# The order of three matrix products per tile: from hi/hi pairs first to equal weights in a row

## The chip, the cores and the metric

The kernel runs on one core of a Trainium2 chip. The metric is the device time of one execution in microseconds (us). An adjacency matrix of 4096 by 4096 float32 streams from the chip's main memory through the core in chunks of 512 by 512 (1 MB each), 192 chunks in all. TensorE (PE) multiplies, ScalarE (ACT) and VectorE (DVE) prepare the operands, and the queue of SyncE (SP) issues the loads.

## The reference

```python
def reference(x, adj, d_list, weight, filt, bias, W_in, W_out):
    # layer 0: U = Vt = adj
    scale = sum(d_list * filt * d_list, axis=0)
    o = adj @ (scale[:, None] * (adj @ (x @ weight))) + bias
    x = layernorm(x + o)
    # layer 1
    a_in  = adj   / where(deg_row > 0, deg_row, 1)
    a_out = adj.T / where(deg_col > 0, deg_col, 1)
    x = layernorm(x + a_in @ x @ W_in + a_out @ x @ W_out)
    return x          # 4096 x 128, float32
```

Four products with the large matrix are needed: two in layer 0 and two in layer 1, each of 4096 x 4096 by 4096 x 128.

## The kernel before, in words

**Precision.** TensorE takes operands in a reduced float32 form. A float32 number is therefore split into a high part and a low part, x = x_hi + x_lo, and for the matrix raw = hi + lo. A product is taken as x_hi hi + x_lo hi + x_hi lo; the fourth term is dropped. ACT makes `hi` by copying `raw` into the reduced form (lines 204 and 207; line 207 also sums the rows). DVE makes `lo` as raw - hi (line 295).

**Tiles.** A chunk has four tiles of 128 x 512 and is worked on in two slabs of two tiles. The x side (128 x 128, `r_hi` and `r_lo` in the code) is the stationary operand, which is loaded as weights; the matrix tile (128 x 512) is streamed. A call of `product` is one chunk: two slabs of six matmuls, all of which add into one accumulator, `accA` or `accB`. There are 256 calls, that is 512 slabs and 3072 large matmuls.

**Stages.** The 192 chunks come in four phases. Phase 1 (64 chunks) makes z = adj x for each block of 512 rows, and as soon as a block's v (z times the layer's weight and scale) is there, the second product v adj goes beside it (`propagate`, `diagonal`). Phase 2 (28 chunks) finishes the second product, and normalises x block by block, with one part of layer 1 (`convolve2`). Phase 3 (64 chunks) is the other direction of layer 1 (`block3`, most of it in a loop that stays a loop in the program). Phase 4 (36 chunks) finishes layer 1, and writes each block of the output (`out_block`, `normalize` on DVE).

**What sets the order.** Each engine has its own order, written out by hand, and waits on counting semaphores. `raw`, `hi` and `lo` are rings of four chunks. The load of chunk n waits until DVE has made `lo` of chunk n-4. ACT's `hi` of chunk n waits for the load and until PE has released chunk n-4 (`s_rel`). DVE's `lo` waits for `hi`. PE waits for `hi` of a slab (`s_hi`) and for its `lo` (`s_lo`). A few small products (lines 485 and 486) and transposes (line 505) stand between the large ones. An instruction carries one wait itself; where it needs two, a separate wait instruction stands ahead of it in PE's program.

Of the kernel before, what the change touches and what calls it, by code (L numbers as in the profile page):

```python
# [12 lines left out]
TPB = 4  # L13
# [10 lines left out]
def graph_kernel(nc, x_t, adj_b, adjT_b, coef_t, W0, bias, W_in, W_out, ident_d, out):  # L24
# [62 lines left out]
    with ExitStack() as ctx:  # L87
        def sb(name, shape, dt=F32):
            return ctx.enter_context(nc.sbuf_tensor(name, shape, dt))
# [8 lines left out]
        hi = sb("hi", [P, RING, TPB, BLK], F32R)  # L98
# [364 lines left out]
        def _(pe):  # L463
            def product(acc, r_hi, r_lo, K, n, first, last, slot=None):

                slot = n % RING if slot is None else slot
                for s in range(SLABS):
                    tiles = range(TPS * s, TPS * s + TPS)
                    pe.wait_ge(s_hi, SLABS * n + (s + 1))
                    for t in tiles:  # L470
                        nc.tensor.matmul(acc, r_hi[:, TPB * K + t], hi[:, slot, t],  # L471
                                         start=(first and t == 0), stop=False)
                        nc.tensor.matmul(acc, r_lo[:, TPB * K + t], hi[:, slot, t], start=False, stop=False)  # L473
                    pe.wait_ge(s_lo, SLABS * n + (s + 1))
                    for t in tiles:
                        mm = nc.tensor.matmul(acc, r_hi[:, TPB * K + t], lo[:, slot, t], start=False,  # L476
                                              stop=(last and t == TPB - 1))
                return mm
# [17 lines left out]
            def diagonal(I):  # L496
                pe.wait_ge(s_v, I + 1)
                product(accB[:, I % 2], v_hi, v_lo, I, NB * I + NB - 1, I == 0, True).then_inc(s_rel, 1)
# [10 lines left out]
            def convolve2(n):  # L509

                J, I = chunks[n]
                pe.wait_ge(s_x1, NB - J)
                if J == NB - 1 and NB - 3 - I > 0:
                    pe.wait_ge(s_ys, NB - 3 - I)
                product(accA[:, I % 2], x_hi, x_lo, J, n, J == NB - 1, J == I + 1).then_inc(s_rel, 1)

            def propagate(n):

                J, I = chunks[n]
                pe.wait_ge(s_v, J + 1)  # L520
                if J == 0 and I >= 2:
                    pe.wait_ge(s_os, I - 1)
                product(accB[:, I % 2], v_hi, v_lo, J, n, J == 0, False).then_inc(s_rel, 1)
# [114 lines left out]
```

## Time and profile before

| | |
|---|---|
| Median of 3 runs | 768.69 us |
| Lowest and highest | 765.61 and 770.52 us |
| Profiled execution, span from first to last instruction | 767.6 us |
| PE busy | 740.5 us (96%), 3352 matmuls, 3352 weight loads |
| DVE busy | 581.9 us (76%) |
| ACT busy | 473.7 us (62%) |
| DMA | 206.48 MB, 269 GB/s on average |
| Granted TensorE clock, mean | 0.995 |

The page gives no other time for the profiled execution than its span, which lies 1.1 us under the median of the runs. A matmul's record begins before the one ahead of it has ended, since they are pipelined; so the distance from one start to the next (called the step below) is what counts, and not the duration. "PEld" rows are the weight loads, which run beside the matmuls. In a timeline, a bracket gives the idle time of the engine ahead of a row and what ended it.

### The profile page before, as it was taken

The page shows a single profiled execution, that of the slowest core. Times are in us where ns is not written, and L with a number is a line of the kernel's source. Part 1 is how long each engine was busy: PE and PEld are TensorE (multiplying, and loading weights), DVE is VectorE, ACT ScalarE, POOL GpSimd, SP SyncE. Part 2 cuts the span into 40 slices and gives each one's busy share as a digit, 9 for nine tenths or more (in the row PEclk, how much of TensorE's full clock was granted, in tenths as well). Part 3 has the DMA queues.
Part 4 walks back from the last instruction along what each step waited for, and adds up shares of the span by engine and source line. Part 5 has one row for each costly group of instructions (what it writes and reads, how often), then busy time and mean ns, then how long its engine had stood idle before and what let it go on. Part 6 is the DMA issues. An engine that isn't in the chain of part 4 may idle for free.

```text
span 767.6 us, 9866 instructions
## 1 busy us (share of the span) xinstructions
PE 740.5 (96%) x3352; PEld 608.2 (79%) x3352; DVE 581.9 (76%) x879; ACT 473.7 (62%) x1209; POOL 0.2 (0%) x4
## 2 busy tenths in 40 slices
PE   5999999999999999899999999999999999989994
PEld 4678888888888888688888888888888888877883
DVE  5897865938373558976566569888889899999986
ACT  6975866646454343333333368898889887556652
POOL 0000000000000000000000000000000000000000
PEclk9999999999999999999999999999999999999999
DMA  9977957656456273355555558899999999799991
GB/s 342 412 301 284 362 196 316 227 212 273 165 202 237 70 315 109 115 215 193 191 189 195 185 199 317 344 367 368 365 360 378 373 348 369 270 313 357 352 346 30
DMA packets 33929, 206.48 MB, mean 269 GB/s; under 512 B 3424, under 2 KB 8288, under 8 KB 9312
## 3 DMA queue, kind: packets, MB, share of 16 engines
q1 hardware_dynamic: 33888, 205.96, 71.4%
q8 instruction: 23, 0.38, 0.2%
q14 instruction: 18, 0.15, 0.0%
HBM read 203.85 MB, written 2.10 MB: 268 GB/s over the span
## 4 chain that ended last, share of the span: by engine, by line
PE 74%; DVE 17%; DMA 5%; ACT 1%; issue 1%; SPq 1%; DVEq 0%; ACTq 0%
PE accB L476 14%; PE accB L471 14%; PE accB L473 14%; PE accA L476 10%; PE accA L471 10%; PE accA L473 10%; DVE lo L295 10%; DMA raw<-in_adjT_b 5%; PE nat L486 2%; DVE rows L363 2%; DVE stats L346 1%; DVE rows L399 1%; ACT hi L207 1%; ACT hi L204 1%; DVE mv L349 1%
## 5 line engine op out<-in xcount | busy, mean ns | idle before, releaser
L295 DVE TENSOR_TENSOR lo<-raw,hi 128x1024 fp32r<-128x1024 f32 x384 | 457.9, 1223 | 101.9 <-ACT hi L207 52.6
L207 ACT ACTIVATE hi<-raw 128x512 fp32r<-128x512 f32 x512 | 315.7, 619 | 101.0 <-PE accB L476 74.5
L471 PE MATMUL accA<-hi,x_hi 128*128 128x512 f32 x512 | 203.4, 397 | 9.2 <-ACT hi L207 8.9
L473 PE MATMUL accA<-hi,x_lo 128*128 128x512 f32 x512 | 200.7, 392 | 0.0
L204 ACT ACTIVATE hi<-raw 128x1024 fp32r<-128x1024 f32 x128 | 127.9, 1051 | 95.7 <-PE accA L476 65.7
L476 PE MATMUL accA<-lo,x_hi 128*128 128x512 f32 x512 | 160.4, 395 | 5.9 <-DVE lo L295 5.8
L471 PEld LDWEIGHTS accA<-hi,x_hi 128*128 128x128 f32 x512 | 96.9, 189 | 31.3 <-issue 8.9
L476 PEld LDWEIGHTS accA<-lo,x_hi 128*128 128x128 f32 x512 | 95.4, 189 | 31.9 <-DVE lo L295 12.7
L473 PEld LDWEIGHTS accA<-hi,x_lo 128*128 128x128 f32 x512 | 97.0, 189 | 19.5
L471 PE MATMUL accB<-hi,v_hi 128*128 128x512 f32 x256 | 100.6, 393 | 0.1
L473 PE MATMUL accB<-hi,v_lo 128*128 128x512 f32 x256 | 100.3, 392 | 0.0
L471 PE MATMUL accB<-hi,x_hi 128*128 128x512 f32 x256 | 100.3, 392 | 0.0
L473 PE MATMUL accB<-hi,x_lo 128*128 128x512 f32 x256 | 99.7, 390 | 0.0
L207 ACT ACTIVATION_READ_ACCUMULATOR hi<-raw 128x1 f32 (+1 forms) x512 | 95.7, 187 | 0.0
L476 PE MATMUL accB<-lo,v_hi 128*128 128x512 f32 x256 | 79.9, 394 | 2.5 <-DVE lo L295 2.5
L476 PE MATMUL accB<-lo,x_hi 128*128 128x512 f32 x256 | 78.9, 389 | 0.0
L476 PEld LDWEIGHTS accB<-lo,v_hi 128*128 128x128 f32 x256 | 48.2, 189 | 13.4 <-DVE lo L295 3.4
L471 PEld LDWEIGHTS accB<-hi,v_hi 128*128 128x128 f32 x256 | 48.3, 189 | 10.9 <-DVE v_lo L326 0.6
L473 PEld LDWEIGHTS accB<-hi,v_lo 128*128 128x128 f32 x256 | 48.4, 189 | 9.8
L476 PEld LDWEIGHTS accB<-lo,x_hi 128*128 128x128 f32 x256 | 48.1, 188 | 10.0
L473 PEld LDWEIGHTS accB<-hi,x_lo 128*128 128x128 f32 x256 | 48.1, 188 | 9.7
L471 PEld LDWEIGHTS accB<-hi,x_hi 128*128 128x128 f32 x256 | 48.1, 188 | 9.7
(54 smaller groups left out, 244.1 us busy)
## 6 DMA issues: line engine op xcount, KB each, us to landing
raw<-in_adjT_b SPq DMA_DIRECT2D x128, 1024.0 KB, 6.0
raw<-in_adj_b SPq DMA_DIRECT2D x64, 1024.0 KB, 6.9
rows<-in_x_t SPq DMA_DIRECT2D x8, 256.0 KB, 9.8
out<-rows SPq DMA_DIRECT2D x8, 256.0 KB, 5.9
coef<-in_coef_t SPq DMA_DIRECT2D x1, 96.0 KB, 7.5
w<-in_W SPq DMA_DIRECT2D x1, 64.0 KB, 7.0
w_in<-in_W_in SPq DMA_DIRECT2D x1, 64.0 KB, 6.9
w_out<-in_W_out SPq DMA_DIRECT2D x1, 64.0 KB, 6.7
```

The source lines that it names most:

```text
L204: last = nc.scalar.activation(hi[:, slot, at], raw[:, slot, at], ACT.Copy)
L207: last = nc.scalar.activation(hi[:, slot, t], raw[:, slot, t], ACT.Copy, accum_out=sums[:, TPB * K + t, bass.ds(C, 1)])
L295: nc.vector.tensor_tensor(lo[:, slot, at], raw[:, slot, at], hi[:, slot, at], ALU.subtract).then_inc(s_lo, 1)
L346: last = nc.vector.bn_stats(stats[:, t], rows[:, TPB * I + t])
L349: last = nc.vector.bn_aggr(mv[:, t], stats[:, t])
L363: last = nc.vector.tensor_scalar(rows[:, TPB * I + t], rows[:, TPB * I + t], mv[:, t, 0:1], rstd[:, t:t + 1], ALU.subtract, ALU.mult)
L399: last = nc.vector.scalar_tensor_tensor(rows[:, r], nat[:, I % 2, P * t:P * t + P], deg[:, 1, r:r + 1], rows[:, r], ALU.mult, ALU.add)
L471: nc.tensor.matmul(acc, r_hi[:, TPB * K + t], hi[:, slot, t], start=(first and t == 0), stop=False)
L473: nc.tensor.matmul(acc, r_lo[:, TPB * K + t], hi[:, slot, t], start=False, stop=False)
L476: mm = nc.tensor.matmul(acc, r_hi[:, TPB * K + t], lo[:, slot, t], start=False, stop=(last and t == TPB - 1))
L486: mm = nc.tensor.matmul(nat[:, b, to], turned[:, b, to], w[:], start=more is None, stop=True)
```

## The change

Within a slab, the two waits now stand together ahead of the first matmul, and the matmuls go tile by tile: x_lo hi, x_hi hi, x_hi lo. The second and the third matmul of a tile have the same stationary operand. The number of matmuls, their operands and their accumulators stay the same, and so does everything on the other engines. Before, only the last two matmuls of a slab stood behind the wait for `lo`.

```diff
                 for s in range(SLABS):
                     tiles = range(TPS * s, TPS * s + TPS)
                     pe.wait_ge(s_hi, SLABS * n + (s + 1))
-                    for t in tiles:
-                        nc.tensor.matmul(acc, r_hi[:, TPB * K + t], hi[:, slot, t],
-                                         start=(first and t == 0), stop=False)
-                        nc.tensor.matmul(acc, r_lo[:, TPB * K + t], hi[:, slot, t], start=False, stop=False)
                     pe.wait_ge(s_lo, SLABS * n + (s + 1))
                     for t in tiles:
+                        nc.tensor.matmul(acc, r_lo[:, TPB * K + t], hi[:, slot, t], start=(first and t == 0), stop=False)
+                        nc.tensor.matmul(acc, r_hi[:, TPB * K + t], hi[:, slot, t],
+                                         start=False, stop=False)
                         mm = nc.tensor.matmul(acc, r_hi[:, TPB * K + t], lo[:, slot, t], start=False,
                                               stop=(last and t == TPB - 1))
```

The first place is PE at the very start of phase 1, the two slabs of the first chunk. A row is one instruction with the accumulator, the streamed and the stationary operand, and the semaphores that it waits for. Before:

```order
L471 MATMUL accA<-hi,x_hi 128x512 [waits hi_ready,x_lo_ready]
L473 MATMUL accA<-hi,x_lo 128x512
L471 MATMUL accA<-hi,x_hi 128x512
L473 MATMUL accA<-hi,x_lo 128x512
L476 MATMUL accA<-lo,x_hi 128x512 [waits lo_ready]
L476 MATMUL accA<-lo,x_hi 128x512
L471 MATMUL accA<-hi,x_hi 128x512 [waits hi_ready]
```

With the change:

```order
L472 MATMUL accA<-hi,x_lo 128x512 [waits lo_ready,hi_ready,x_lo_ready]
L473 MATMUL accA<-hi,x_hi 128x512
L475 MATMUL accA<-lo,x_hi 128x512
L472 MATMUL accA<-hi,x_lo 128x512
L473 MATMUL accA<-hi,x_hi 128x512
L475 MATMUL accA<-lo,x_hi 128x512
L472 MATMUL accA<-hi,x_lo 128x512 [waits lo_ready,hi_ready]
```

The wait for `lo` has moved ahead of four matmuls that do not read `lo`, and the slab's first matmul has two waits or more where it had one.

The second place is PE in the middle of phase 1 (150.7 us of the trace), where a product of z ends and `propagate` begins. Before, its first matmul had two waits already:

```order
L476 MATMUL accA<-lo,x_hi 128x512 [waits lo_ready]
L476 MATMUL accA<-lo,x_hi 128x512
L471 MATMUL accB<-hi,v_hi 128x512 [waits hi_ready,v_ready]
L473 MATMUL accB<-hi,v_lo 128x512
L471 MATMUL accB<-hi,v_hi 128x512
```

With the change:

```order
L475 MATMUL accA<-lo,x_hi 128x512
L472 MATMUL accB<-hi,v_lo 128x512 [waits lo_ready,hi_ready,v_ready]
L473 MATMUL accB<-hi,v_hi 128x512
L475 MATMUL accB<-lo,v_hi 128x512
L472 MATMUL accB<-hi,v_lo 128x512
```

Here the first matmul has one wait more than before, and nothing else at the boundary has moved.

## Rows read from the trace of the kernel before

**Rows 1.** The page: busy time, share of the span and instructions by engine.

```profile
PE 740.5 (96%) x3352; PEld 608.2 (79%) x3352; DVE 581.9 (76%) x879; ACT 473.7 (62%) x1209; POOL 0.2 (0%) x4
```

**Rows 2.** Windows: stretch, length, busy us by engine (instructions), clock, DMA share, GB/s.

```profile
0.00:45.00 45.00, 35.00 (x131) 24.35 (x132) 33.13 (x42) 34.06 (x98) 0.20 (x4) 1.00 0.98 379
45.00:305.00 260.00, 260.00 (x1179) 215.95 (x1177) 170.93 (x215) 145.69 (x441) 0.00 (x0) 1.00 0.60 231
305.00:330.00 25.00, 22.24 (x90) 17.44 (x90) 22.29 (x59) 7.28 (x10) 0.00 (x0) 0.93 0.38 130
330.00:485.00 155.00, 155.00 (x697) 128.44 (x696) 102.69 (x173) 76.23 (x150) 0.00 (x0) 1.00 0.59 216
485.00:640.00 155.00, 155.00 (x712) 129.33 (x711) 137.10 (x142) 137.72 (x427) 0.00 (x0) 1.00 0.95 362
640.00:768.00 128.00, 113.26 (x551) 92.74 (x549) 115.77 (x251) 72.75 (x85) 0.00 (x0) 0.98 0.78 285
```

**Rows 3.** Groups of instructions: busy us, mean ns, idle time before them and its enders.

```profile
L295 DVE TENSOR_TENSOR lo<-raw,hi 128x1024 fp32r<-128x1024 f32 x384 | 457.9, 1223 | 101.9 <-ACT hi L207 52.6 <-ACT hi L204 47.7
L471 PE MATMUL accA<-hi,x_hi 128*128 128x512 f32 x512 | 203.4, 397 | 9.2 <-ACT hi L207 8.9 <-DVE x_lo L381 0.2
L476 PE MATMUL accA<-lo,x_hi 128*128 128x512 f32 x512 | 160.4, 395 | 5.9 <-DVE lo L295 5.8
L473 PEld LDWEIGHTS accA<-hi,x_lo 128*128 128x128 f32 x512 | 97.0, 189 | 19.5
```

**Rows 4.** Timeline of PE at 150 us: start, duration, engine, line, operands, count.

```profile
150.25 0.62 PE L476 MATMUL accA<-lo,x_hi 128*128 128x512 f32 x2
150.71 0.39 PE L471 MATMUL accB<-hi,v_hi 128*128 128x512 f32 x1
150.93 0.39 PE L473 MATMUL accB<-hi,v_lo 128*128 128x512 f32 x1
```

**Rows 5.** Timeline of PE, chunks 68 and 69 (314 to 325 us).

```profile
314.13 0.39 PE L471 MATMUL accB<-hi,v_hi 128*128 128x512 f32 x1
...
315.52 0.74 PE L476 MATMUL accB<-lo,v_hi 128*128 128x512 f32 x2 [0.32 <-DVE lo L295]
...
323.50 1.04 PE L476 MATMUL accB<-lo,v_hi 128*128 128x512 f32 x2 [2.21 <-DVE lo L295]
324.34 0.63 PE L471 MATMUL accB<-hi,v_hi 128*128 128x512 f32 x1
324.77 0.63 PE L473 MATMUL accB<-hi,v_lo 128*128 128x512 f32 x1
```

**Rows 6.** Timeline of PE, chunk 8 and the first small product.

```profile
38.89 0.61 PE L476 MATMUL accA<-lo,x_hi 128*128 128x512 f32 x2
40.35 1.16 PE L486 MATMUL nat<-w,turned 128*128 128x128 f32 x8 [0.85 <-ACT turned L223]
```

**Rows 7.** Timeline of PE, the first matmul of chunk 11.

```profile
50.01 0.39 PE L471 MATMUL accA<-hi,x_hi 128*128 128x512 f32 x1
```

**Rows 8.** Timeline of DVE, `lo` of chunks 11 and 12.

```profile
48.91 4.91 DVE L295 TENSOR_TENSOR lo<-raw,hi 128x1024 fp32r<-128x1024 f32 x4 [0.73 <-ACT hi L207]
```

**Rows 9.** Timeline of PE, the first matmul of chunk 147 (phase 3).

```profile
612.35 0.39 PE L471 MATMUL accB<-hi,x_hi 128*128 128x512 f32 x1
```

**Rows 10.** Timeline of DVE, `lo` of chunks 147 to 149.

```profile
611.52 7.42 DVE L295 TENSOR_TENSOR lo<-raw,hi 128x1024 fp32r<-128x1024 f32 x6 [1.67 <-ACT hi L207]
```

**Rows 11.** Waits of 330 to 485 us: total us, times, longest.

```profile
ACT hi L204 <- PE accA L476: 62.3, 17, 7.1
```

**Rows 12.** Waits of 640 us to the end.

```profile
PE accA L476 <- DVE lo L295: 5.8, 8, 1.3
DVE rows L399 <- PE nat L486: 3.8, 1, 3.8
```

**Rows 13.** Timeline of PE, the last wait for `lo` (chunk 189).

```profile
750.32 0.74 PE L476 MATMUL accA<-lo,x_hi 128*128 128x512 f32 x2 [1.29 <-DVE lo L295]
750.90 0.40 PE L471 MATMUL accA<-hi,x_hi 128*128 128x512 f32 x1
```

## The prediction

> **What bounds the kernel now.** I read the page's busy shares first, then the windows by stage, then the groups, the timeline of PE, and last the waits. The reader is to see that PE is busy 96% of the span, with one weight load for each matmul [rows 1]. In three stages, 45 to 305, 330 to 485 and 485 to 640 us, PE never idles [rows 2]; they hold 570 of 768 us. So most of the time is PE's step, the distance between two starts. At 150 us two matmuls begin at 150.25 and 150.48 and the next at 150.71 and 150.93 [rows 4]: 0.227 us each. The stages without idle time on PE move only if this step moves. Elsewhere others supply the work: DMA at a share of 0.98 up to 45 us, DVE busy 22.3 of 25 us around 315 us and 115.8 of 128 us behind 640 us [rows 2]. There PE catches up with `lo` and stands still until DVE delivers.
>
> **Part 1: equal weights in a row.** In each tile two neighbouring matmuls now have the same stationary operand, 1024 pairs in all (256 products of four tiles). The built program keeps a weight load for every matmul, as before; the change reorders loads, it removes none. A load takes 189 ns [rows 3] beside a matmul, and the step is 227 ns, so it is hidden with 38 ns to spare. 3072 large matmuls by 227 ns are 697 us. At the low clock the step is 427 ns (324.34 to 324.77) [rows 5], which is 512 columns at 1.2 GHz with nothing on top; at 2.4 GHz 512 columns are 213 ns, so some 14 ns of the full-clock step are not streaming. Whether they belong to the change of weights no row tells, because no two neighbours had equal weights before. The bounds: 0 if a load of equal weights is a load like any other, 1024 x 14 ns = 14 us gained if the pair saves all of it. I take 0, since the load is issued all the same, and since the step is one and the same whether the neighbour has another accumulator (150.48 to 150.71) or not [rows 4].
>
> [...]
>
> **Part 2: two waits ahead of a slab.** Each of the 512 slabs now has a separate wait instruction on PE in front of its first matmul. The nearest row is a boundary that had one before: the first matmul of `propagate` at 150.71 waits for `hi` and for v, and stands 0.23 us behind its neighbour [rows 4], the same step as anywhere. Where the semaphore is long up, the price is 0. The upper bound is what a matmul pays that finds its weights unloaded: at 750.32 and behind it, the pair takes 0.58 us up to the next start [rows 13] instead of 2 x 0.227 = 0.454, so 0.126 us. Over 512 slabs that would be 65 us. I take 0, from the row that is the same thing.
>
> **Part 3: the wait for `lo` moves ahead of four matmuls.** Where `lo` comes long before the slab, this costs nothing. Where PE stood at the wait, the four matmuls that it had done before the wait are now done after it: 4 x 0.227 = 0.91 us late. It is paid once for a stretch of dense work behind the stall, not at each stall: at the next stall the date is DVE's, and a PE that comes up to 0.9 us late there stands less before it. So I look for the last stall ahead of each stage in which PE has no idle time.
>
> - *Start, up to 45 us.* PE meets late `lo` in nearly each slab of chunks 0 to 8, but then stands 0.85 us for ACT at 40.35, with its last matmul of chunk 8 begun at 39.1 [rows 6]. The lateness there is below four matmuls, as the second slab waits less (about 0.7 us), and this pause takes it. 0.
> - *Phase 1.* DVE's row of four `lo` from 48.91 gives the first at 48.91 + 1.23 = 50.14 [rows 8]; PE began that chunk at 50.01 [rows 7]. PE now waits 0.13 us. This pattern stands once per block of eight chunks, four times in all (50, 78, 109, 143 us); later blocks have more than 0.4 us in hand. Behind it PE has no idle time, and the others wait for PE, so nothing gives it back: 4 x 0.13 = 0.5 us.
> - *Phase 2.* Chunk 68 starts at 314.13 and its `lo` comes by 315.5; the delay goes into the stall that ends at 323.50 [rows 5]. There the four matmuls of chunk 69 go behind the stall: +0.9 us. The clock falls in this pause in both kernels, which is 2.21 us long before and about as long after, since the work ahead of it is 0.8 us late and the four matmuls of chunk 69 no longer fill it. In the dense stage that follows ACT waits for PE, 62.3 us in 17 waits [rows 11]; it is delayed with PE, and PE with it. +0.9 stays. If the four matmuls went at 427 ns it would be 1.7.
> - *Phase 3.* `lo` is just in time. The worst slab begins at 612.35 with its `lo` at 611.52 + 1.24 = 612.76 [rows 9, 10], 0.4 us late; twelve or so slabs have 0 to 0.4. A wait here puts PE behind, and the next `lo` then finds it late enough. PE meets DVE's stall behind 640 us anyway. 0; at most 0.9, if each of the four blocks with a late slab kept its own (0.1 + 0.2 + 0.4 + 0.2).
> - *Phase 4.* Eight stalls of PE on `lo`, 5.8 us together, and DVE waits for PE only once, at the very end; no wait of ACT's `hi` for PE is among the stage's waits [rows 12]. So DVE's dates stand and only the last stall counts: chunk 189 at 750.32 [rows 13]. Behind it all is PE's to the end, with ACT and DVE finishing the last block after PE. +0.9.
>
> Sum: 0.5 + 0.9 + 0.9 = 2.3 us. The profiled execution would take 767.6 + 2.3 = 769.9 us; its span is 1.1 us under the median of the runs, so the forecast for the median is 768.69 + 2.3 = 771.0 us.
>
> **Rivals.**
>
> *A, the forecast: the order costs three late starts.* 771.0. Its own bounds: below, nothing (768.7, if the small waits are given back); above, 2.3 + 0.8 (low clock) + 0.9 (phase 3) = 4.0, so 772.7. The runs before spread from 765.6 to 770.5, so a median of a few runs can lie 2 us off. Chance 0.83.
>
> *B, equal weights pay.* The second load of a pair costs no changeover, and the step falls from 227 towards 213 ns in one of three. For it: 14 ns of the step are not explained by streaming. Against it: the program loads again, and the load is hidden. 1024 x 14 = 14 us gained, plus 2.3 of waits: 757. Chance 0.06.
>
> *C, slower: the extra wait instruction keeps PE from loading ahead.* Its place is the head of every slab. It decides from the point at which PE's program no longer runs ahead of the array: the weights are then loaded only once the wait has passed. At 0.126 us a slab, 65 us: 834; if it hit one slab in five, 13 us and 784. Against it: the step at 150.71 [rows 4], where such an instruction stood already; but before there was one every 12 matmuls or more, and now one every six. The small matmuls speak against it too: eight of them take 1.16 us at 40.35 [rows 6], with the last one's duration of 0.28 some 0.11 us each with their loads, so six matmuls can be issued in 0.7 of the 1.36 us that a slab takes. Chance 0.05. [...] The trace at 150.71 shows no cost.
>
> *D, the stalls add up.* In phase 4, PE's release comes 0.9 us later; if ACT's `hi` of the chunk four on hung on it, each of the eight stalls would pass 0.9 us on to DVE: 7 us, plus 2.3: 778. Against it: no such wait in the stage [rows 12]. Chance 0.06.
>
> **How the numbers follow.** The likeliest case gives 771.0. A with the scatter of a median reaches from 766.5 to 775; B, C and D hold 0.17, which is what may be left out, so 766.5 to 775.5 stands. A measurement of this kernel tells 1% (7.7 us) from no change. Faster by over that (under 761.0): B, 0.06. Slower (over 776.4): C and D and a little of A, 0.11. Within: 0.83.
>
> **What would show it.** After the change, the step in dense stretches must still be 227 ns, at the x_hi hi to x_hi lo pair as at others (B wrong, 213 to 216 there if right), and at the head of a slab (C wrong). The matmul count and the load count stay at 3352. The wait rows of PE for `lo` must move to the x_lo hi matmul and hold more time in all, while the idle time before L475 vanishes. The stall of chunk 69 must be followed by six matmuls instead of two, and the last small product must start about 0.9 us later against DVE's last `lo`. Waits of ACT's `hi` for PE in phase 4 would speak for D. The forecast is wrong if the step of the dense stages differs by more than 2 ns, which alone is 6 us.

## The result, and the profile after

| | before | change |
|---|---|---|
| Median of 7 runs, us | 767.96 | 772.68 |
| Lowest and highest, us | 765.61 and 770.52 | 771.48 and 774.64 |
| Span of the profiled execution, us | 767.6 | 772.2 |
| Time of the change to before, 95% interval | | 1.0069 [1.0048, 1.0089] |

The change makes the kernel 4.7 us slower, 0.7%. Run again on another chip it stood at 1.0098 [1.0080, 1.0117] (E8 below). The forecast was 2.3 us slower, 771.0 us, in a range from 766.5 to 775.5: the direction and the range hold, and the growth is half of the measured one. Two executions among those of the experiments, one of the kernel before (4264.91 us) and one of E4 (2656.75 us), lie far outside and are in no ratio below.

The page's first line of the changed kernel, then the windows by stage. They answer to [rows 1, 2]; columns as there.

```profile
PE 740.1 (96%) x3352; PEld 607.5 (79%) x3352; DVE 581.0 (75%) x879; ACT 473.6 (61%) x1209; POOL 0.2 (0%) x4
```

```profile
0.00:45.00 45.00, 33.09 (x133) 25.13 (x134) 33.61 (x43) 34.06 (x98) 0.20 (x4) 1.00 0.97 379
45.00:305.00 260.00, 259.52 (x1173) 214.41 (x1172) 169.40 (x212) 145.79 (x441) 0.00 (x0) 1.00 0.61 231
305.00:330.00 25.00, 21.19 (x86) 16.41 (x85) 23.02 (x61) 7.28 (x10) 0.00 (x0) 0.93 0.38 126
330.00:485.00 155.00, 155.00 (x695) 128.34 (x694) 102.34 (x174) 74.12 (x144) 0.00 (x0) 1.00 0.59 211
485.00:640.00 155.00, 154.56 (x704) 127.06 (x704) 135.05 (x137) 138.39 (x433) 0.00 (x0) 1.00 0.96 363
```

Matmuls and weight loads are as many as before, 3352. The page counts 10294 instructions in all, 428 more than the 9866 before; all of them are separate wait instructions of PE (51 ns each), of which there were 130 and are now 558. Before, the wait for `hi` ahead of a slab stood 101 times as an instruction of its own (L469). Now L470 stands ahead of each of the 512 slabs and L469 is left 17 times, so 529 against 101; 101 of the 512 hold two waits. No weight load has more than one wait in either trace: 1056 have one before, 544 with the change. That, and not a rule for every instruction, is what the traces show of where a wait can stand. PE's busy time is the same as before, 740.1 against 740.5 us. What grew is idle time and steps longer than 227 ns: 45 to 305 us had 1179 matmuls and now has 1173, 485 to 640 us had 712 and now has 704. The stage from 330 to 485 us, where PE is far behind DVE, is as dense as before (695 against 697; the two are a matter of where the window cuts).

The equal weights first. The timeline of PE at 150 us in the changed kernel, which answers to [rows 4]:

```profile
150.26 0.39 PE L475 MATMUL accA<-lo,x_hi 128*128 128x512 f32 x1
150.49 0.39 PE L472 MATMUL accA<-hi,x_lo 128*128 128x512 f32 x1
150.71 0.39 PE L473 MATMUL accA<-hi,x_hi 128*128 128x512 f32 x1
150.94 0.39 PE L475 MATMUL accA<-lo,x_hi 128*128 128x512 f32 x1
```

L473 to L475 is the pair with equal weights: 0.23 us, like the two others. The 217 such pairs from 330 to 480 us have a median step of 227 ns, as every other place in the slab has.

Where the time went is read from the start of the same matmul in both traces. The shift is the later start in the changed kernel. Each trace is one execution, so a shift at one place carries the scatter of all that lies ahead of it; what counts is by how much it grows within a stretch.

| place | before, us | change, us | shift, us |
|---|---|---|---|
| chunk 9 (behind the first small product) | 41.26 | 40.74 | -0.5 |
| phase 1, behind the four late heads | 296.07 | 297.20 | +1.2 |
| behind the stall of chunk 69 | 326.90 | 329.17 | +2.3 |
| phase 3, before the first loss | 441 to 496 | | +2.1 |
| phase 3, its end | 635.02 | 639.13 | +4.1 |
| phase 4, behind its first DVE stall | 644.31 | 648.10 | +3.8 |
| last large matmul | 757.5 | 762.1 | +4.6 |

**Phase 1.** A head is the first matmul of a slab, and it is late where it waits for `lo`. PE and then DVE around chunk 11, against [rows 7, 8]:

```profile
49.23 0.39 PE L475 MATMUL accA<-lo,x_hi 128*128 128x512 f32 x1
49.73 0.47 PE L472 MATMUL accA<-hi,x_lo 128*128 128x512 f32 x1
50.04 0.39 PE L473 MATMUL accA<-hi,x_hi 128*128 128x512 f32 x1
50.27 0.40 PE L475 MATMUL accA<-lo,x_hi 128*128 128x512 f32 x1
```

```profile
48.36 4.91 DVE L295 TENSOR_TENSOR lo<-raw,hi 128x1024 fp32r<-128x1024 f32 x4 [0.74 <-ACT hi L207]
```

The head's step is 0.50 us (49.23 to 49.73) and the next 0.31, instead of 0.227 each: 0.36 us lost, and 0.4 with the slightly long steps behind. Lateness of `lo` is only 0.13 of it. The first `lo` is ready at 48.36 + 1.23 = 49.59, and the matmul starts 0.145 us behind that. The same head stands at 78.3, 109.5 and 143.6 us. Four times 0.4 is the growth from -0.5 to +1.2 in the table (1.7 us).

**Phase 2.** The stall of chunk 69, against [rows 5]:

```profile
324.76 0.62 PE L472 MATMUL accB<-hi,v_lo 128*128 128x512 f32 x1 [2.26 <-DVE lo L295]
325.18 0.63 PE L473 MATMUL accB<-hi,v_hi 128*128 128x512 f32 x1
```

All six matmuls of the slab stand behind the stall, where two stood before; the low clock is there in both profiles (step 0.43 before and 0.42 here, at a granted share of 0.50 from 323.8 to 327.1 us before and from 324.95 to 328.3 us here). Right behind the stall the shift has grown by 1.1 us, and by 1.0 where it settles (+2.1 in the table).

**Phase 3.** Here is what I had not foreseen: 2.0 us are lost between 501 and 635 us. DVE around 556 us and the head of PE that waited for it:

```profile
556.34 1.12 DVE L388 SCALAR_TENSOR_TENSOR rows<-nat,deg,rows 128x128 f32 x4 [1.11 <-PE nat L485]
557.38 9.16 DVE L295 TENSOR_TENSOR lo<-raw,hi 128x1024 fp32r<-128x1024 f32 x8
```

```profile
558.42 0.39 PE L475 MATMUL accB<-lo,x_hi 128*128 128x512 f32 x1
558.74 0.47 PE L472 MATMUL accB<-hi,x_lo 128*128 128x512 f32 x1
559.05 0.40 PE L473 MATMUL accB<-hi,x_hi 128*128 128x512 f32 x1
```

DVE's `h_block` (L388) waits 1.11 us for PE's small product, its `lo` comes at 557.38 + 1.22 = 558.60, and PE's head waits for that. PE waits for DVE, which has waited for PE. The waits of 485 to 640 us say how often, the first line from the kernel before, the others with the change:

```profile
DVE rows L388 <- PE nat L486: 5.9, 5, 2.0
```

```profile
DVE rows L388 <- PE nat L485: 8.6, 7, 2.0
ACT hi L207 <- PE accB L475: 1.3, 2, 0.9
```

Eight heads of this phase lose time, and they are of two kinds. Six of them stand right behind an `h_block` and lose 0.86 us together; the same six lose 0.86 us in E8's profile too, though the waits of `h_block` differ there. The two others, at 569.85 and 593.35 us, lose 0.88 us (four such heads and 1.96 us in E8). Their `lo` waited for ACT's `hi`, and ACT for a load. ACT and DVE of chunk 131:

```profile
567.11 0.63 ACT L207 ACTIVATE hi<-raw 128x512 fp32r<-128x512 f32 x1 [2.12 <-DMA raw<-in_adj_b]
568.48 3.68 DVE L295 TENSOR_TENSOR lo<-raw,hi 128x1024 fp32r<-128x1024 f32 x3 [1.93 <-ACT hi L207]
```

That load is late for the same reason, one turn of the ring on: it is issued at 559.76, 0.03 us behind the end of `lo` of chunk 127, which is the one behind the `h_block` shown above; that of the other head follows the next `h_block` in the same way.

**Phase 4.** The last wait for `lo` ends at 754.08, against 750.32 in [rows 13]; from it on 36 large matmuls are left, the three last chunks whole; before, 32 were left, since four of chunk 189 had run ahead of the stall. The last large matmul starts 2.50 us behind the end of DVE's last `lo`, against 1.58 before.

```profile
754.08 0.47 PE L472 MATMUL accA<-hi,x_lo 128*128 128x512 f32 x1 [0.53 <-DVE lo L295]
754.38 0.40 PE L473 MATMUL accA<-hi,x_hi 128*128 128x512 f32 x1
```

### The profile page after: what moved, and what is told of

It is laid out like the page before. It is cut to its first block, busy times and chain, and to the rows that moved or that the text cites. A ratio compares the mean times of both kernels' runs of the same rounds, so it can differ in the third digit from the quotient of the medians.

```text
span 772.2 us, 10294 instructions
## 1 busy us (share of the span) xinstructions
PE 740.1 (96%) x3352; PEld 607.5 (79%) x3352; DVE 581.0 (75%) x879; ACT 473.6 (61%) x1209; POOL 0.2 (0%) x4
## 4 chain that ended last, share of the span: by engine, by line
PE 74%; DVE 16%; DMA 6%; issue 2%; ACT 1%; SPq 1%; DVEq 0%; ACTq 0%
PE accB L472 14%; PE accB L473 14%; PE accB L475 14%; PE accA L472 10%; PE accA L475 10%; PE accA L473 10%; DVE lo L295 9%; DMA raw<-in_adjT_b 5%; PE nat L485 2%; DVE rows L363 2%; DVE stats L346 1%; DVE rows L399 1%; DMA raw<-in_adj_b 1%; ACT hi L207 1%; ACT hi L204 1%
## 5 line engine op out<-in xcount | busy, mean ns | idle before, releaser
L472 PE MATMUL accA<-hi,x_lo 128*128 128x512 f32 x512 | 203.8, 398 | 19.4 <-DVE lo L295 16.5
L475 PE MATMUL accA<-lo,x_hi 128*128 128x512 f32 x512 | 200.3, 391 | 0.0
L473 PE MATMUL accA<-hi,x_hi 128*128 128x512 f32 x512 | 200.1, 391 | 0.0
L475 PEld LDWEIGHTS accA<-lo,x_hi 128*128 128x128 f32 x512 | 96.5, 189 | 20.7
L473 PEld LDWEIGHTS accA<-hi,x_hi 128*128 128x128 f32 x512 | 96.7, 189 | 19.0
L473 PE MATMUL accB<-hi,v_hi 128*128 128x512 f32 x256 | 100.4, 392 | 0.0
L475 PE MATMUL accB<-lo,v_hi 128*128 128x512 f32 x256 | 100.3, 392 | 0.0
L475 PE MATMUL accB<-lo,x_hi 128*128 128x512 f32 x256 | 99.7, 389 | 0.0
L473 PE MATMUL accB<-hi,x_hi 128*128 128x512 f32 x256 | 99.7, 389 | 0.0
L475 PEld LDWEIGHTS accB<-lo,v_hi 128*128 128x128 f32 x256 | 48.5, 189 | 10.3
L473 PEld LDWEIGHTS accB<-hi,v_hi 128*128 128x128 f32 x256 | 48.4, 189 | 9.8
L475 PEld LDWEIGHTS accB<-lo,x_hi 128*128 128x128 f32 x256 | 48.1, 188 | 10.2
L473 PEld LDWEIGHTS accB<-hi,x_hi 128*128 128x128 f32 x256 | 48.1, 188 | 9.4
```

## The experiments

The theory T: the order by equal weights is worth nothing; the 4.7 us are the wait for `lo` that moved ahead of the slab, by matmuls that stand behind a stall, by heads that cost more than their lateness, and by the ring of waits in phase 3 (PE waits for DVE, and DVE for PE). The rivals: R1, the order itself acts on the time. R2, the added wait instruction costs by itself. R3, the losses of phase 3 are late loads. All diffs are against the kernel before, unless said. Intervals are 95%.

**E1: the old order, both waits ahead.**

```diff
                     pe.wait_ge(s_hi, SLABS * n + (s + 1))
+                    pe.wait_ge(s_lo, SLABS * n + (s + 1))
                     for t in tiles:
...
-                    pe.wait_ge(s_lo, SLABS * n + (s + 1))
```

> The order of the matmuls is the old one (hi pairs first, no equal weights in a row), only the wait for lo is moved ahead of the slab. If the waits alone are the cause: the same as the change, 772.7 us (+4.7 on 768.0), with the same late heads in phase 1 (a step of about 0.51 us at 49.7 us). If the order by equal weights costs or saves something by itself, this run differs from the change by that: over 2 us would count. If the cause is only the extra wait instruction and not the place of the wait for lo: also +4.7, which e4 separates.

Measured: 772.71 us, 1.0078 [1.0050, 1.0107]. With no equal weights in a row, the time is the change's. The head at 49.2 us has a step of 0.51 here too. R1 falls as far as it would explain the loss.

**E2: the order of the change, one wait.** Against the change:

```diff
-                    pe.wait_ge(s_hi, SLABS * n + (s + 1))
                     pe.wait_ge(s_lo, SLABS * n + (s + 1))
```

> The order of the change, but one wait per slab (for lo alone, which implies hi), so that no separate wait instruction stands ahead of the slab. If the separate instruction is what makes a late head dear (the matmul began 145 ns behind lo's end, against 55 ns before the change), the distance at stalls falls from 145 to about 55 ns, the four late heads of phase 1 cost less, and the time is 770.5 to 772, 1 to 2 us under the change. If the place of the wait is all of it, 772.7. Not under 770, since the four matmuls still stand behind the last stall.

Measured: 771.21 us, 1.0055 [1.0035, 1.0075], 1.5 us under E1 on the same chip. The order differs between the two as well, but E3 below gives it no worth. The intervals of the two overlap, so the trace decides on the mechanism. PE at the same head:

```profile
49.83 0.39 PE L474 MATMUL accA<-lo,x_hi 128*128 128x512 f32 x1
50.25 0.50 PE L471 MATMUL accA<-hi,x_lo 128*128 128x512 f32 x1
50.58 0.39 PE L472 MATMUL accA<-hi,x_hi 128*128 128x512 f32 x1
```

The step is 0.42 and the next 0.33, together 0.75 instead of 0.81 us. The start behind lo's end is 54 to 55 ns at the heads that really wait for `lo` alone, and 145 to 147 ns where a separate instruction holds one of the waits. So the separate wait costs 0.06 us net at a head that really waits; a wait by itself costs about 0.16 us on top of the lateness (0.75 - 0.454, less 0.136 that `lo` is late). The weights are loaded only then. A dense head has its load one step ahead (the kernel before, chunk 11: load at 49.78, matmul at 50.01), but here it starts with the matmul; first E2, then the change, where a wait instruction of 0.05 us (49.63 to 49.68) lies between the end of `lo` (49.59) and the load:

```profile
50.24 0.19 PEld L471 LDWEIGHTS accA<-hi,x_lo 128*128 128x128 f32 x1 [0.45 <-DVE lo L295]
```

```profile
49.70 0.19 PEld L472 LDWEIGHTS accA<-hi,x_lo 128*128 128x128 f32 x1 [0.51 <-ACT hi L207]
```

The bracket of the second names ACT's `hi`, which had been done since 48.36 at the latest, as DVE's `lo` began then; the wait that ended last is the one for `lo`.

How far PE's program runs ahead of the array is in the change's trace too. Taken in order, L470 of a slab starts 3.4 us (median of 112 slabs, 0.97 at the least) before the slab's first weight load from 330 to 485 us, and by 150 us it has run 98 times, while 95 slabs have begun. Where it stands 0.5 us or more ahead, from 45 to 640 us, the median step to the head is 227 ns (371 slabs). At 49.63 us it is 0.07 us ahead, and the head is late.

Part of the 1.5 us lies outside the trace. The record has for each execution the core's span beside its time. Time less span is 1.8 us (median) for the kernel before on each of the three chips where it was run beside the experiments, and for each version with its 9866 instructions (E2, E3, E5, E6, E9, E10, E11). It is 2.0 us for the change, 2.3 for E1, 2.1 for E4, 2.6 for E7 and 2.7 for E8, the five with 10294 instructions, and it differs by about 1 us between their executions. So the separate wait instructions also cost 0.2 to 0.9 us before the first or behind the last instruction; by what is open. Of the 1.5 us between E1 and E2, 1.0 are span.

**E3: equal weights, with the wait where it was.**

```diff
                     for t in tiles:
-                        nc.tensor.matmul(acc, r_hi[:, TPB * K + t], hi[:, slot, t],
+                        nc.tensor.matmul(acc, r_lo[:, TPB * K + t], hi[:, slot, t],
                                          start=(first and t == 0), stop=False)
-                        nc.tensor.matmul(acc, r_lo[:, TPB * K + t], hi[:, slot, t], start=False, stop=False)
+                        nc.tensor.matmul(acc, r_hi[:, TPB * K + t], hi[:, slot, t], start=False, stop=False)
                     pe.wait_ge(s_lo, SLABS * n + (s + 1))
-                    for t in tiles:
+                    for t in reversed(tiles):
...
```

> The waits stand where they stood before the change, four matmuls ahead of the wait for lo; but the slab's fourth and fifth matmul have the same weights (x_hi of its second tile), 512 pairs. If equal weights are worth nothing: 768.0 us, the step of the pair 227 ns. If equal weights save the changeover: 512 x 14 ns = 7 us less, 761.

Measured: 766.75 us against 766.89, 0.9991 [0.9974, 1.0009]. The 7 us are not there; the interval leaves room for 2 us of gain at most for the 512 pairs. PE at 150 us:

```profile
150.05 0.39 PE L471 MATMUL accA<-hi,x_lo 128*128 128x512 f32 x1
150.28 0.39 PE L473 MATMUL accA<-hi,x_hi 128*128 128x512 f32 x1
150.50 0.61 PE L476 MATMUL accA<-lo,x_hi 128*128 128x512 f32 x2
150.96 0.39 PE L471 MATMUL accA<-hi,x_lo 128*128 128x512 f32 x1
```

The pair with equal weights is 150.28 to 150.50, a step like the others.

**E4: one more wait that never waits.**

```diff
                     pe.wait_ge(s_hi, SLABS * n + (s + 1))
+                    if not (isinstance(n, int) and n + s == 0):
+                        pe.wait_ge(s_lo, SLABS * n + s)
```

> The kernel before with one more wait at the head of each slab, for the lo of the slab before, which PE has already waited for: it never waits, it only adds the separate instruction. If such an instruction is free where its semaphore is up: 768.0 us, +0.5 at most. If it costs by itself: up to all of the +4.7 us.

Measured: 767.76 us against 766.89, 1.0018 [1.0001, 1.0035]. That is more than nothing by the interval, and over the 0.5 us that I had allowed; it is 0.9 us by the medians. In the trace the dense stages lose nothing: the start of the same matmul is shifted by -0.84 us at 50 us and by -0.83 us at 311 us. So R2 is not the 4.7 us, as far as the wait never waits. Of the 0.9 us, 0.3 lie outside the span (2.1 against 1.8 us); where the 0.6 would lie that the median spans differ by, the trace does not say.

**E5: the order of the change, the wait where `lo` is first read.** Against the change:

```diff
-                    pe.wait_ge(s_lo, SLABS * n + (s + 1))
                     for t in tiles:
...
                         nc.tensor.matmul(acc, r_hi[:, TPB * K + t], hi[:, slot, t],
                                          start=False, stop=False)
+                        if t == TPS * s:
+                            pe.wait_ge(s_lo, SLABS * n + (s + 1))
```

> The order of the change, but the wait for lo stands where lo is first read, ahead of the slab's third matmul: two matmuls run before it, not none (the change) and not four (before). If what counts is how many matmuls stand behind the wait: the four late heads of phase 1 vanish (lo is 0.13 us behind the head there, two matmuls cover 0.45 us), phase 3 loses nothing, and behind the stalls of chunks 69 and 189 two matmuls stand that stood before them, 0.45 us each: 768 + 0.9, against + 4.7 to + 5.8 for the change. If any wait inside the slab costs the same, as much as the change.

Measured: 768.03 us against 766.64, 1.0030 [1.0011, 1.0049]. The direction is as expected, two matmuls ahead lie between none and four. The size (1.4 us by the medians, 2.3 by the ratio) is above 0.9, but the interval, 0.8 to 3.8 us, holds 0.9. The four heads are gone: the shift to before is 0.14 us at 50 us and at 143 us alike. The two stalls cost what was expected (at the second, the last large matmul starts 2.15 us behind DVE's last `lo` instead of 1.58). A loss that was not expected stands at the end of phase 3: two late `lo`, at 635 and 641 us, move the shift by 1.2 us; how much of it is kept, the scatter of phase 4 hides.

**E6: eight matmuls ahead of the wait.**

```diff
+                for s in range(SLABS):
+                    tiles = range(TPS * s, TPS * s + TPS)
                     pe.wait_ge(s_lo, SLABS * n + (s + 1))
                     for t in tiles:
...
```

> The other way: the eight hi matmuls of both slabs first, then the four with lo, so that eight stand ahead of the first wait for lo. If lateness behind the stalls is the mechanism, this is faster than before by what PE has done ahead of the stalls of chunks 69 and 189: lo of the second slab comes 1.2 us behind the first, so 0.4 to 0.9 us each, 1 to 1.5 us in all, 766 to 767. If the stalls do not set the end, 768.0.

Measured: 766.66 us against 766.64, 0.9999 [0.9981, 1.0016]. A miss by the medians: no gain that can be told, though the interval does not exclude 1 us. The trace shows why little is to be had. PE at the stall of chunk 69:

```profile
323.57 0.73 PE L478 MATMUL accB<-lo,v_hi 128*128 128x512 f32 x2 [1.57 <-DVE lo L295]
324.70 0.73 PE L478 MATMUL accB<-lo,v_hi 128*128 128x512 f32 x2 [0.40 <-DVE lo L295]
```

With all eight done, PE has two matmuls until the second slab's `lo`, which takes DVE 1.2 us more, and stands again. The expectation left this second wait out. The gain is 0.2 to 0.3 us a stall. Behind chunk 69 the shift has fallen by 1.8 us, of which 1.6 are the clock that did not fall in this execution, and behind chunk 189 the last large matmul starts 1.31 us behind DVE's last `lo`, against 1.58.

**E7: the change with `h_block` later.** Against the change:

```diff
-                    elif k == 2:
+                    elif k == 4:
                         h_block(J - 1, 1 - b)
```

> The change, with DVE's h_block in phase 3 two chunks later (after the fifth lo of a block instead of the third). With the change DVE waited for PE's small products 7 times (8.6 us) there, and PE lost 1.4 us in phase 3. Theory: DVE's wait for PE ties the dates of lo to PE, so that every late head stays lost; without that wait the late heads of phase 3 vanish and the time is 1 to 1.5 us under the change. Rival: the heads of phase 3 are late because the load of raw is late, and the wait has no part in it: the same time as the change.

Measured: 771.05 us, 1.0068 [1.0049, 1.0087], beside E8's 773.10 us, 1.0098 [1.0080, 1.0117], on the same chip: 2.1 us less, and as much by the median spans; the executions reach from 769.82 to 772.77 and from 772.51 to 775.25. The trace shows it more sharply. Windows of E7, then of E8, 485 to 640 us:

```profile
485.00:640.00 155.00, 155.00 (x712) 129.28 (x711) 141.03 (x144) 139.13 (x429) 0.00 (x0) 1.00 0.97 371
```

```profile
485.00:640.00 155.00, 153.97 (x698) 125.85 (x697) 136.11 (x137) 135.85 (x425) 0.00 (x0) 1.00 0.95 358
```

E7 has 712 matmuls, as many as before [rows 2], and no idle time of PE; from 441 to 635 us its shift to before does not move at all (0.01 us), while E8's grows by 3.1 us. DVE after the fifth `lo` in E7, where no wait stands any more:

```profile
552.11 6.15 DVE L295 TENSOR_TENSOR lo<-raw,hi 128x1024 fp32r<-128x1024 f32 x5
558.17 1.12 DVE L388 SCALAR_TENSOR_TENSOR rows<-nat,deg,rows 128x128 f32 x4
559.21 7.36 DVE L295 TENSOR_TENSOR lo<-raw,hi 128x1024 fp32r<-128x1024 f32 x6
```

R3 falls as a cause of its own: the chunks and their order are the same, and the loss is gone. Late loads are a link of the chain, though, since E7 also moves the loads: that of chunk 131 is issued at 555.82 instead of 559.76 us. What E7 does not part is `h_block`'s wait for PE from its own work of 1.1 us, since both move together. For the wait speaks that in each of the six late heads of the first kind it lasted 0.57 us or more, and none of them lost over 0.19 us; without it their `lo` would have been in time.

**E8: the change again.**

> The change itself, unaltered, on the chip of the other three, to compare with: + 4.7 us on the kernel before, within 1.5 us.

Measured: 773.10 us, 1.0098 [1.0080, 1.0117]. By the medians that is +6.5 us, 1.8 more than the first time and a little over the 1.5 that I had allowed. Of the 6.5 us, 5.7 are span and 0.9 lie outside it. The two profiles differ in phase 3, where 3.1 us are lost here and 2.0 there, in phase 4, where the shift falls by 0.6 us here (2.75 to 2.18) and grows by 0.8 there, and in the clock (last section); how much of the difference of the medians each is stays open.

**E9: the kernel before with `h_block` later**, the edit of E7.

> The kernel before with DVE's h_block in phase 3 two chunks later, as in e7. In the kernel before PE had no idle time in phase 3, so taking DVE's wait for PE away there should give nothing by itself: 766.6 us, 0 to 1 faster through phase 4, which it enters with DVE further ahead. If it gives 2 us or more, e7's gain over the change was not the change's late heads but a gain of h_block's place in any kernel.

Measured: 766.28 us against 767.25, 0.9991 [0.9972, 1.0009]. The edit is worth nothing that can be told to the kernel before, so what it cured in E7 was the change's own loss.

**E10: the change with E2's and E7's edits.**

> The change with both cures: one wait per slab (e2) and h_block later (e7). If the two terms are apart and add up, e7's 771.1 less what e2 saved (about 1.5 us): 769.5. What then stays over the kernel before, some 3 us, is what the four matmuls behind the stalls of chunks 69 and 189 and the lateness of lo in phase 1 cost. If the two cure the same thing: 771.

Measured: 769.82 us, 1.0031 [1.0016, 1.0047]. It lies 0.37 points of the ratio under E7, so the two terms are apart, as far as ratios of two chips can be compared. Some 2.4 us stay over before, of which the stalls of chunks 69 and 189 account for 1.8.

**E11: eight ahead and `h_block` later.**

> Eight hi matmuls ahead of the first wait for lo (e6) with h_block later: the version to which the runs so far point. e6 alone measured the same as before. 765.5 to 766.6 us, 0 to 1 us faster than before; slower is not expected.

Measured: 765.24 us against 767.25, 0.9971 [0.9953, 0.9988]. This version beats the kernel before by 0.3%, which is 2.0 us by the medians, more than the 1 us expected. Each of its edits alone measured nothing (E6, E9), and why the two together give more is not shown.

## Why the prediction was right or wrong, point by point

- *Equal weights are worth 0 (part 1): right.* The load stays, the step is 227 ns at the pair in the change and in E3, and the 14 ns that I could not explain are no matter of equal or other weights. E3 leaves 2 us at most. The 14 ns, and with them the 1.2 and 2.4 GHz, were my estimate from [rows 5]: 512 columns in 427 ns are 1.2 a ns at a granted share of 0.50, so 213 ns at full share, if nothing but streaming is in the slow step. No run shows a step of 213 ns, nor the 216 that I put beside it for rival B: the shortest between two large matmuls in the 13 profiles is 223 ns, and the pair goes at 227, with its load issued again.
- *The extra wait instruction is free where its semaphore is up (part 2): right in dense stretches*, as E4's unmoved shift (-0.84 us at 50 us, -0.83 at 311 us) and the change's 371 heads at a median of 227 ns show. The step that failed is that I priced it for that case alone, and carried the 0 over to heads that wait. There the start comes 145 ns behind `lo` instead of 54, and the step behind it is long in both cases (0.31 and 0.33 us). My own upper bound, 0.126 us for a late pair, belonged into each head of part 3, and was no upper bound: it left out the time from the end of `lo` to the start. Rival C had this place right, at the few heads that wait (0.07 us from wait to load at 49.63 us) and not at each slab (a median of 3.4 us from 330 to 485 us). That the instructions also lengthen the time outside the span was in no part of the prediction.
- *Phase 1: the place and the count right, the size wrong.* Four heads, 0.13 us late each, cost 0.4 us and not 0.13: 1.6 to 1.7 us instead of 0.5. This term is 1.1 of the 2.4 us that the forecast lacks.
- *Phase 2: right.* 0.9 was forecast and 1.0 measured (from 1.2 to 2.1 in the table). The low clock behind the stall is no part of it, since both profiles have it; that it fell in both is chance (last section).
- *Phase 3: the step that failed.* I wrote that a wait puts PE behind and that the next `lo` then finds it late enough. That needs DVE's dates to be free of PE, and `h_block` ties them. The waits of the kernel before held it, DVE's L388 for PE's small product, 5.9 us in 5 waits, and the prediction gave them no weight; it asks for DVE's waits on PE in phase 4 alone. I had put 0.9 as the most; it was 2.0 by 635 us and 1.7 net behind the first stall of phase 4, and 3.1 in E8. E7 and E9 show that the place of `h_block` is the cause; that it acts by its wait is read from the trace.
- *Phase 4: the mechanism right.* Between DVE's last `lo` and the last large matmul 0.9 us are added, as forecast: 2.5 us in the change, E1, E2, E7, E8 and E10, against 1.5 to 1.6 in before, E3, E4 and E9. The shift over the whole phase, +0.8, agrees with 0.9 in this profile by luck, for in E8's it is -0.6: DVE's own dates move by more than that from one execution to the next. There is no wait of ACT's `hi` for PE as a tie. Rival D fell in phase 4, but its mechanism is what happened one phase earlier.
- *The start:* 0 forecast, -0.5 in this profile, and -1.0 and +0.1 in those of E8 and E2. It is scatter: E9, whose phase 1 is the kernel before's own, stands at +1.9 at the same place.
- *The number.* 771.0 lies near 772.7 in part by luck. The forecast took its base from 3 runs, 768.69, and 7 runs gave 767.96; and single executions of the kernel before reach from 763.9 to 770.5 us beside E5 to E8, so the 767.6 of one profile says little on the median. The median span of the kernel before was 764.9 to 765.4 us on the three chips of the experiments.
- *What is open.* What the extra instructions do outside the span, and the two late `lo` at the end of phase 3 in E5. The account is good for the change, and not good to 1 us for its neighbours.

## What to carry to other kernels

Where a wait is moved ahead of work that does not need it, count for each head not only how late the data is, but also what a start from standstill costs (here 0.16 us, and 0.22 with a separate wait instruction), and look for every wait by which the supplier in turn waits for this engine: it decides whether a delay is given back at the next stall or kept. Equal stationary operands in a row were worth nothing here, where each matmul issues its own load and that load is hidden (189 ns in a step of 227). A wait belongs directly ahead of the first instruction that reads the data.

## What the runs showed of the hardware that I had not expected

- In E2 a matmul that waits for one semaphore started 54 to 55 ns behind the end of DVE's instruction; in E2 and the change one with a separate wait instruction ahead started 145 to 147 ns behind it. The step that followed was 335 to 341 ns in the first case and 304 to 312 in the second, against 227, at a granted share of 1.00.
- The five versions with 428 more wait instructions take 2.0 to 2.7 us (medians) beyond the core's span, all others 1.8.
- Behind the stall of chunk 69 (PE idle 2.2 to 2.3 us) the granted share of the clock fell to 0.50 for 3.41 us in five of the 13 profiles (before, the change, E1, E4, E10: the window of 305 to 330 us at 0.93) and stayed at 1.00 in eight, six of them with the same pause and two, E6 and E11, with 1.6 us. In E3 and E9 it was at 0.50 at 42 to 44 us instead, behind a pause of 2.2 to 2.3 us ahead of the first small product. In E7:

```profile
324.23 0.47 PE L472 MATMUL accB<-hi,v_lo 128*128 128x512 f32 x1 [2.26 <-DVE lo L295]
324.54 0.39 PE L473 MATMUL accB<-hi,v_hi 128*128 128x512 f32 x1
324.77 0.40 PE L475 MATMUL accB<-lo,v_hi 128*128 128x512 f32 x1
```

  The step is 0.23 here and 0.43 in the change's profile behind a pause of the same 2.26 us. Between E7 or E8 and the change that is 1.6 us of the span, which no edit explains.
